# A decoder layer on one core: the orders of all engines rearranged, the second batch projected in the prologue

## The reference

```python
# self-attention: 16 heads of 64, two null keys and values per head, q and k normalized, ALiBi, causal
xn = (x - mu) * rsqrt(var + eps) * gamma
q, k, v = heads(xn @ w_q), heads(xn @ w_k), heads(xn @ w_v)
k, v = concat([null_k, k]), concat([null_v, v])
q, k = l2norm(q) * q_scale, l2norm(k) * k_scale
attn = softmax(masked(8.0 * q @ k.T - slope[h] * distance))
x1 = layernorm(x + (attn @ v) @ w_out)
# cross-attention: 16 heads of 8, 64 context rows per batch
x2 = layernorm(x1 + mha(x1, ctx, wq, wk, wv) @ wo.T + bo)
# two linear layers in a row, other weights for every pair of batches
x3 = layernorm(x2 + (x2 @ W1[g].T + b1[g]) @ W2[g].T + b2[g])
```

## Time and profile before

| | |
|---|---|
| median of three runs | 1048.96 us (1045.95 to 1051.13) |
| profiled execution, its own time | 1049.69 us |
| its span, first to last instruction | 1047.6 us |
| mean granted TensorE clock | 0.912 of full speed |
| busy share: TensorE, VectorE, ScalarE, GpSimd | 82%, 74%, 64%, 41% |

### The profile page before, as it was taken

How to read it: one execution, slowest core, us unless ns; L and a number is a source line. 1 busy time by engine, 2 the same in 40 slices (tenths; PEclk the granted TensorE clock), 3 DMA queues, 4 the chain that set the end, 5 groups by cost and what they waited for, 6 DMA issues and landing times. The chain is left out here.

```text
span 1047.6 us, 19543 instructions
## 1 busy us (share of the span) xinstructions
PE 856.9 (82%) x6469; PEld 609.2 (58%) x6469; DVE 772.6 (74%) x2496; ACT 671.2 (64%) x2002; POOL 424.7 (41%) x356
## 2 busy tenths in 40 slices
PE   6778788797888879787887979888797978887763
PEld 4546566475655647565565747556474755656542
DVE  6554677878788787878778787887878787676744
ACT  5485768567585856758485765848576684756532
POOL 1134272625345162535416362542626254162511
PEclk8789999899999989989999998989999898989875
DMA  5000000000100001000100001000010000000000
GB/s 183 6 6 2 11 21 12 6 12 1 27 11 6 12 6 32 1 11 7 26 12 6 12 6 29 4 6 12 6 32 6 7 1 26 6 6 6 7 1 10
DMA packets 26418, 15.62 MB, mean 15 GB/s; under 512 B 4304, under 2 KB 25552, under 8 KB 26320
## 3 DMA queue, kind: packets, MB, share of 16 engines
q1 hardware_dynamic: 26320, 14.38, 4.8%
HBM read 12.27 MB, written 2.10 MB: 14 GB/s over the span
## 5 line engine op out<-in xcount | busy, mean ns | idle before, releaser
L1580 POOL TENSOR_TENSOR pr<-pr,rden 128x512 f32<-128x512 f32 x192 | 193.2, 1040 | 138.5 <-DVE rden L1037 138.5
L1347 ACT ACTIVATE pr<-pr,nmin 128x256 f32<-128x256 f32 (+1 forms) x512 | 225.5, 443 | 13.6 <-DVE nmin L1022 13.5
L1022 DVE CUSTOM_DVE_ANT_0 pr<-psS,alibi,nullmin 128x256 f32<-128x256 f32 (+1 forms) x512 | 180.5, 413 | 16.6 <-PE psS L553 16.6
L553 PE MATMUL psS<-kT,qT 64*128 64x256 f32 (+1 forms) x1024 | 121.6, 368 | 33.5 <-DVE nmin L1022 33.3
L1377 ACT ACTIVATE xp<-xp 128x1024 f32<-128x1024 f32 x32 | 33.8, 1057 | 152.2 <-DVE xp L1082 152.2
L1571 POOL TENSOR_TENSOR qk<-qk,rn 128x1024 f32<-128x1024 f32 x64 | 120.5, 1906 | 25.1 <-DVE rn L883 25.1
L575 PE MATMUL psT<-ident,pr 128*128 128x128 f32 x768 | 126.7, 293 | 1.5 <-POOL pr L1580 1.5
L978 DVE TENSOR_REDUCE ssq<-sq 128x16 f32<-128x1024 f32 x64 | 77.9, 1218 | 62.6 <-ACT sq L1313 62.2
L553 PEld LDWEIGHTS psS<-kT,qT 64*128 64x128 f32 x1024 | 85.3, 201 | 63.3 <-issue 60.1
L1613 POOL TENSOR_TENSOR x1b<-x,bo 128x256 f32<-128x256 f32 x16 | 11.7, 734 | 244.6 <-DVE r L1094 222.7
L1305 ACT ACTIVATE qk<-psJ 128x512 f32<-128x512 f32 x128 | 76.0, 596 | 48.7 <-PE psJ L443 48.5
(11 more groups left out here) (145 smaller groups left out, 1762.1 us busy)
## 6 DMA issues: line engine op xcount, KB each, us to landing
w1s<-w1b SPq DMA_DIRECT2D x8, 258.0 KB, 3.1
xin<-x SPq DMA_DIRECT2D x16, 128.0 KB, 2.2
xres<-x SPq DMA_DIRECT2D x16, 128.0 KB, 2.1
w2s<-w2T SPq DMA_DIRECT2D x8, 256.0 KB, 3.5
out<-x SPq DMA_DIRECT2D x16, 128.0 KB, 1.8
pr<-w_kv SPq DMA_DIRECT2D x2, 512.0 KB, 5.5
pr<-w_q SPq DMA_DIRECT2D x1, 512.0 KB, 3.9
wo<-wout SPq DMA_DIRECT2D x1, 512.0 KB, 6.0
```

The source lines that it names most:

```text
L553: mm = pe.matmul(psS[score_bank(t, c)][:, keys * j:keys * (j + 1)], qT[r, h // 2, P * t:P * (t + 1)], kT[r, h // 2, 0:keys], start=True, s ...
L1022: dve.tensor_tensor_reduce(pr[t][:, h, :], psS[score_bank(t, c)][:, keys * j:keys * (j + 1)], alibi[:, h, SEQ - keys:SEQ], 1.0, nullmin[:, ...
L1347: act.activation(pr[t][:, h, :], pr[t][:, h, :], ACT.Exp, bias=nmin[:, t, h:h + 1], scale=-1.0, accum_out=dparts[:, t, h, 0:1]).then_inc(e ...
L1580: pool.tensor_tensor(pr[t][:, hs, :], pr[t][:, hs, :], rden[:, t, hs].unsqueeze(2).broadcast_to([P, heads, P * (t + 1)]), ALU.mult).then_i ...
```

## The change

Nothing is computed otherwise. What is changed is the order in which the engines' queues hold the steps, and what the prologue does:

- VectorE: `ln3_begin` and `ln3_end` stand earlier among the first tile's masks; `ln4_end` stands ahead of `denominators(i, 1)`, not behind; `ln1_end` stands ahead of the cross denominators; the second tile's sums of squares of batch i + 1 and its `norms` stand among the masks of the second tile; half of the ALiBi rows are made here.
- ScalarE: seeds, the q and k copies and the squares of batch i + 2 stand earlier; `x1T` is copied first.
- GpSimd: `norm_qk(i + 1, 0)` stands behind `norm_probs(i, 0)` (it stood ahead of it), `norm_qk(i + 1, 1)` at the end of the iteration.
- TensorE: `project_qk(i + 2, 1)` to `(i + 2, 4)` stand one or two steps earlier.
- Batch 1's `ln1`, projections, copies, squares and first norms stand in the prologue on all engines, where they stood in iteration 0. Its input has a buffer of its own (`xin1`, in the memory of `r2`) and its own DMA, and `p` holds for iteration 0 too.

```diff
-            return i + 3 < NB, i + 2 < NB, i + 1 < NB, i >= 1, i >= 2, 1 <= i < NB - 1
+            return i + 3 < NB, i + 2 < NB, i + 1 < NB, i >= 1, i >= 2, i + 1 < NB
...
             sp.dma_start(wqk_raw[:, HD:2 * HD], w_kv[:, 0:HD]).then_inc(wk_loaded, 16)
+            sp.dma_start(xin1[:], x_dram[:, 1]).then_inc(xin1_loaded, 16)
...
             turn_null_keys()
+            xn_turn(1)
+            for c in range(4):
+                project_qk(1, c)
             merged_nulls()
             null_values()
             project_nulls(0)
+            for c in range(4, QK_CHUNKS):
+                project_qk(1, c)
             project_v(0, 0)
...
                 if i == 0:
-                    for k in range(2, QK_CHUNKS):
-                        project_qk(1, k)
-                    project_nulls(1)
                     context_kv()
...
+                    if f and k == 4:
+                        project_qk(i + 2, 1)
...
             def iteration(i, w, g):
                 d, f, a, c, e, p = stages(i)
-                if i == 0:
-                    split_xnT(1)
                 if e:
                     add_y2(i - 2)
+                    ln3_begin(i - 2)
+                need(dve, probsT_ready, PC * (i - 1) + TILE_PC[0])
+                mask_scores(i, 0, (0, 1))
+                if e:
+                    ln3_end(i - 2)
+                mask_scores(i, 0, (2, 3))
+                null_shift(i, 0)
                 if p:
                     sum_squares(i + 1, 1, 0)
-                need(dve, probsT_ready, PC * (i - 1) + TILE_PC[0])
-                mask_scores(i, 0, (0, 1))
-                if p:
-                    sum_squares(i + 1, 1, 1)
-                    floor_squares(1)
-                if e:
-                    ln3_begin(i - 2)
-                mask_scores(i, 0, (2, 3))
-                null_shift(i, 0)
-                if e:
-                    ln3_end(i - 2)
-                if p:
-                    norms(i + 1, 1)
-                if i == 0:
-                    ln1_begin(2)
-                    ln1_end(2)
                 need(dve, probsT_ready, PC * i)
                 for k in range(8):
                     mask_scores(i, 1, (k,))
                     if k == 1:
+                        if p:
+                            sum_squares(i + 1, 1, 1)
+                            floor_squares(1)
                         denominators(i, 0)
+                    if k == 4 and p:
+                        norms(i + 1, 1)
...
                 null_shift(i, 1)
-                denominators(i, 1)
                 if e:
                     ln4_end(i - 2)
+                denominators(i, 1)
                 if c:
                     cross_shift(i - 1, 0)
                     cross_shift(i - 1, 1)
...
                 if f:
                     split_xnT(i + 2)
+                if d:
+                    ln1_begin(i + 3)
...
-                if d:
-                    ln1_begin(i + 3)
-                copy_pT(i, 6)
+                if d:
+                    ln1_end(i + 3)
+                if a:
+                    null_scores(i + 1)
                 if c:
                     cross_denominators(i - 1, 0)
...
-                copy_pT(i, 5)
-                copy_pnT(i, 1)
-                if c:
-                    cross_exponentials(i - 1, 1)
-                if f:
-                    copy_qk(i + 2, 0)
                 if d:
                     ln_seed("ln1", (0, 1), i + 4)
-                copy_pT(i, 7)
+                copy_pnT(i, 1)
+                copy_pT(i, 5)
+                if f:
+                    copy_qk(i + 2, 0)
+                if c:
+                    cross_exponentials(i - 1, 1)
...
                 if c:
                     x1_plus_bias(i - 1)
-                if p:
-                    norm_qk(i + 1, 0)
                 if e:
                     x2_plus_bias(i - 2, (i - 2) // 2)
                 norm_probs(i, 0)
                 if p:
-                    norm_qk(i + 1, 1)
+                    norm_qk(i + 1, 0)
                 if c:
                     spread_values(i)
                 norm_probs(i, 1)
...
                 spread_keys(i)
                 if c:
                     norm_cross(i - 1)
+                if p:
+                    norm_qk(i + 1, 1)
```

More of the change, by code:

```diff
@@ L210, in program @@
         r3 = r2
+        xin1 = r2
         x3 = sb("x3", [P, NT, P])
@@ L716, in _ @@
             project_nulls(0)
+            for c in range(4, QK_CHUNKS):
+                project_qk(1, c)
             project_v(0, 0)
             project_v(0, 1)
[L719 to L723, removed]
+            for c in range(4):
+                turn_qk(0, 2 * c)
+                turn_qk(0, 2 * c + 1)
+                if c < 2:
+                    project_v(0, 2 + c)
+            project_nulls(1)
             def iteration(i, w, g):
                 d, f, a, c, e, p = stages(i)
-                if i == 0:
-                    xn_turn(1)
                 scores(i, 0, 0)
@@ L802, in iteration @@
                         if f:
[L803 to L805 removed]
+                            project_qk(i + 2, 4)
                 if c:
@@ L896, in ln_end, with make_alibi @@
                 return last
+            def make_alibi(heads):
+                dve.wait_ge(a_loaded, 16)
+                for h in heads:
+                    dve.tensor_scalar(alibi[:, h, :], dist, float(slopes()[h]), None, ALU.mult).then_inc(alibi_ready_dve, 1)
             def scale_rows():
@@ L961, in ln1_begin @@
             def ln1_begin(n):
-                dve.wait_ge(xin_loaded, 16 * (n + 1))
-                ln_begin("ln1", xin, (0, 1), n + 1)
+                if n == 1:
+                    dve.wait_ge(xin1_loaded, 16)
+                else:
+                    dve.wait_ge(xin_loaded, 16 * max(n, 1))
+                ln_begin("ln1", xin1 if n == 1 else xin, (0, 1), n + 1)
             def ln1_end(n):
-                ln_end("ln1", xin, xn, (0, 1), n + 1).then_inc(xn_ready, 1)
+                ln_end("ln1", xin1 if n == 1 else xin, xn, (0, 1), n + 1).then_inc(xn_ready, 1)
             def split_xnT(n):
@@ L1123, in _ @@
             split_wqk(3)
+            ln1_begin(1)
             null_squares()
             norm_null_keys()
+            ln1_end(1)
             sum_squares(0, 0, 0)
-            split_wv(0)
+            split_xnT(1)
+            make_alibi(range(8, H))
             sum_squares(0, 0, 1)
             floor_squares(0)
+            norms(0, 0)
+            split_wv(0)
+            sum_squares(0, 1, 0)
             split_wv(1)
-            norms(0, 0)
-            sum_squares(0, 1, 0)
-            split_wn()
             sum_squares(0, 1, 1)
             floor_squares(1)
+            split_wn()
             norms(0, 1)
@@ L1410, in _ @@
             copy_qk(0, 3)
-            null_keys_seed()
             copy_qk(0, 4)
             copy_qk(0, 5)
+            null_keys_seed()
             square_qk(0, 0, 0)
             copy_qk(0, 6)
+            ln_seed("ln1", (0, 1), 2)
             square_qk(0, 0, 1)
@@ L1420, in _ @@
             square_qk(0, 1, 0)
+            for c in range(4):
+                copy_qk(1, c)
             square_qk(0, 1, 1)
@@ L1423, in _ @@
             copy_nullraw(0)
-            make_alibi(range(8, H))
+            copy_qk(1, 4)
+            copy_qk(1, 5)
+            square_qk(1, 0, 0)
+            copy_qk(1, 6)
+            copy_qk(1, 7)
+            square_qk(1, 0, 1)
             copy_v(0, 0)
             copy_v(0, 1)
+            ln_seed("ln1", (0, 1), 3)
+            qk_seed(1, 0)
             act.wait_ge(kscale_ready, 1)
@@ L1431, in _ @@
                     copy_v(0, 2 + k)
-            ln_seed("ln1", (0, 1), 2)
+            square_qk(1, 1, 0)
+            square_qk(1, 1, 1)
+            copy_nullraw(1)
             def iteration(i, w, g):
                 d, f, a, c, e, p = stages(i)
+                if e:
+                    ln_seed("ln3", (0, 1), i - 1)
+                if c:
+                    copy_x1T(i - 1)
                 if a:
                     copy_v(i + 1, 0)
-                exponentials(i, 0, (0,))
-                if c:
-                    copy_x1T(i - 1)
-                exponentials(i, 0, (1,))
-                if i == 0:
-                    copy_qk(1, 0)
-                    copy_qk(1, 1)
+                exponentials(i, 0, (0, 1))
                 if a:
                     copy_v(i + 1, 1)
-                if p:
-                    qk_seed(i + 1, 1)
-                if e:
-                    ln_seed("ln3", (0, 1), i - 1)
                 if c:
@@ L1640, in iteration @@
                 if i == 0:
-                    norm_qk(1, 0)
-                    norm_qk(1, 1)
                     spread_values(i)
```

85 lines of the change are left out of this document (32 added, 53 removed).

## The result

The changed kernel takes 976.16 us, the median of four runs (973.33 to 977.13), against 1050.05 for the kernel before; the ratio is 0.930, with a 95% interval of 0.926 to 0.933. The forecast was 980 us, from 952 to 1015. The profiled execution has a span of 975.3 us, 72.3 less than before.

| stretch | before | after | difference | forecast |
|---|---|---|---|---|
| up to the first scores of iteration 2 | 172.8 | 164.4 | -8.4 | -4.5 |
| first halves, iterations 2 to 13, mean | 24.98 | 25.30 | 12 x 0.32 = +3.9 | 0 |
| second halves, even ones, mean | 35.26 | 30.82 | 6 x -4.44 = -26.6 | with the odd ones |
| second halves, odd ones, mean | 36.71 | 31.46 | 6 x -5.25 = -31.5 | -58.8 |
| from the first scores of iteration 14 to the end | 143.3 | 133.6 | -9.7 | -6.8 |

The account below looks back on a forecast made before the run. No engine is busy throughout; the one large loss was TensorE's 3.40 us wait for xp, as GpSimd holds VectorE's ln4_end. Gains 58.8 + 6.8 + 0 + 4.5 = 70.1 us from 1049.7 give 980 us, range 952 to 1015.

Parts of the forecast that it names:

- The main step: Second halves: ln4_end ahead of denominators(1) ends TensorE's wait for xp and slow running; 4.9 us, 58.8 over iterations 2 to 13.
- 4.40 and 5.85: Odd second halves' excess over iteration 1: 4.40 us, or 5.85 without iteration 1's own 1.45 us wait at merge_ffn.
- I take the 3.40 alone for each: Iterations 14 and 15, no projections behind the wait: only TensorE's 3.40 us wait each is gained, 6.8 us.
- The first half: Masks and exponentials: VectorE gains by moved steps, is held about as long, ScalarE ends as now; 0 us.
- the lower end of -5 us: First halves: ScalarE sets the half, 24.4 against 24.8 us, gaining 0.4 each; -5 us over thirteen iterations.
- the rule quoted in the prediction: VectorE and GpSimd share a port pair exclusively; operations with two SBUF inputs need it, the second to come is blocked.
- The prologue: Batch 1's work moved from iteration 0 to the prologue: 16.8 us gone, 12.3 added, net gain 4.5, ends 12 and 0.
- I take 12.3: Prologue: eight projections, the null projection and the turn of xn add 12.3 us of TensorE, the full amount.
- the lower bound of 4.9: Prologue: least time added, 4.9 us, if TensorE's 7.4 us of idle time took up part of the 12.3.
- The other side of the sum: Iteration 0: the 11.7 us context delay and VectorE's 5.05 us wait for the ln1 seed go, 16.8 us.
- The third rival: GpSimd late: norm_qk(i+1,1) behind norm_cross makes TensorE's turn_qk(i+1,4) wait; 1056 us, chance 0.05.
- the lower of the prediction's two values: GpSimd's end after norm_probs(1): 23.2 us, or 20.5 if the cross denominators come 2.7 us sooner.

Follow-up runs that it names:

- norms_late: Kernel after with norms(i + 1, 1) moved from among the second tile's masks to behind ln4_end, ahead of denominators(i, 1): 940.2 us, ratio 0.896.
- qk0_early: Kernel after with norm_qk(i + 1, 0) ahead of norm_probs(i, 0) on GpSimd, VectorE's order untouched: 943.3 us, ratio 0.901.
- prologue_alone: Prologue of the kernel after with the iterations of the kernel before, without their i == 0 pieces for batch 1: 1034.5 us, ratio 0.986.
- ln4_alone: Kernel before with one edit, ln4_end ahead of denominators(i, 1): 985.7 us, ratio 0.939.
- add_wait: Kernel before in its own order, with GpSimd's norm_probs(i, 1) also waiting until ln4_end(i - 2) is done: 992.9 us, ratio 0.948.
- qk_split: Kernel after with each norm_qk in four GpSimd instructions of 512 columns in place of two of 1024: 960.2 us, ratio 0.917.

## Why the prediction was right

*The main step.* GpSimd holds `ln4_end`, that delays `cross_shift`, and TensorE stands still and then runs slowly: shown by three kernels, one that moves the step, one that moves it back, and one that leaves it and keeps GpSimd away. The 4.9 us an iteration were 4.84 in the full change (58.1 us over twelve iterations, 58.8 forecast) and 4.52 with the move alone. In the odd iterations the full change gives 0.90 us more than the move, and TensorE's wait at `merge_ffn` is gone from it, as the prediction had it when it chose between 4.40 and 5.85. In the even ones it gives 0.25 us less, and why is not shown.

*The end.* From iteration 14 on the gain was 9.7 us, 6.8 forecast. "I take the 3.40 alone for each" was too little: iteration 14's second half fell by 4.7 us (29.68 to 24.96), and the stretch behind iteration 15's first half by 4.6 (66.71 to 62.14). TensorE had run slowly there too: `cross_scores(1)` of iteration 14 took 2.08 us before and 1.13 after.

*The first half.* The sum of nearly nothing was right, for a reason that was only half right. The prediction expected VectorE to be held for about as long as it gains by the steps that moved behind it; so it was. But it took a half of about 24.4 us for the shortest that ScalarE allows. The runs show a half of 23.1 us where `norms` is not held (norms_late, qk0_early), so the new order had 1.9 us an iteration to give (24.98 - 23.07), and the hold took 2.2 (25.30 - 23.07). Over twelve iterations that is 23 us won and 27 lost: that the two nearly cancel is luck, since neither size was forecast. (One half of 26.64 us, iteration 13, lifts the mean before from 24.83 to 24.98.) The step that failed is the lower end of -5 us, 0.4 an iteration: it went by iteration 1's 23.4 with 1 us added for a copy and two seeds, and the half can be shorter than that.

The Trainium skill, page "SBUF — State Buffer", section "Who interferes with whom", says besides the rule quoted in the prediction that a tensor_scalar may take the second port pair too, and that a tensor_reduce on this chip never does. The traces agree: the tensor_scalar of `ln4_end` was held (2.03 for 0.60 us), the sum of squares beside `norm_qk` was not (1.20, qk0_early). What the page says of the other side, that GpSimd blocks when it comes second, no run here shows: the eight `norm_probs` took 8.02 to 8.05 us with a held instruction beside them and without.

*The prologue.* The mechanism was right, the size not: 4.5 us were forecast for prologue and iteration 0, and prologue_alone measured 15 (13.0 up to iteration 1 in its trace). The term that failed is "I take 12.3": iteration 0 began 5.7 us later there. That is near the lower bound of 4.9, but not for the bound's reason. TensorE's idle time took up nothing: from 16.5 us to the first scores it was idle for 7.4 us before (busy for 19.39 of 26.83) and 7.5 in prologue_alone (24.98 of 32.53). What was too high is the price of 1.28 us for each projection, taken where the clock was low. Two of the passes in prologue_alone, of which a projection has three, in stretches with a granted clock of 0.50 (20.50 to 23.40) and 1.00 (36.66 to 39.96):

```profile
22.77 0.63 PE L445 MATMUL psJ<-wqk_hi,xnT_lo 128*128 128x512 f32 x1
...
39.56 0.40 PE L445 MATMUL psJ<-wqk_hi,xnT_lo 128*128 128x512 f32 x1
```

So a part of the gain hangs on the granted clock, which differs between kernels that hold the same prologue. In qk0_early, with the same prologue, the granted clock from 16.5 us to the first scores is 0.69, as before the change, where prologue_alone has 0.79; TensorE is busy there for 29.89 us, and iteration 0 begins 11.3 us later than before, near the 12.3. Over the seven kernels with this prologue it is 5.7 to 11.6, and 8.1 in the kernel after. The other side of the sum was nearly right: iteration 0 lost 18.7 us in its trace (73.84 to 55.16), 16.8 forecast. In the kernel after, the context is copied directly behind `aoT`, as the prediction said, at 75.7 us (ScalarE's timeline of iteration 0):

```profile
75.18 0.58 ACT L1336 ACTIVATE aoT<-psY 128x512 f32<-128x512 f32 x1
75.66 1.25 ACT L1297 ACTIVATE kTx<-psJ,xb 128x512 f32<-128x512 f32 x2
```

There iteration 1 begins 9.9 us sooner than before, not 13.0: iteration 0 starts 2.4 us later than in prologue_alone and its first half is 1.8 us longer; its `norms` is held too.

*The sum.* That 72.3 us came so near to 70.1 is in part luck too: the first halves lost 3.9 us that were forecast as nothing, and the stretch up to iteration 2 and the end gave 3.9 and 2.9 us more than forecast.

*The third rival*, GpSimd late at the turn of q and k, did not come about: `norm_qk(i + 1, 1)` ends at 549.29 in iteration 8, 20.5 us behind `norm_probs(1)`, the lower of the prediction's two values.

## What to carry to other kernels

A small VectorE instruction that runs three to ten times its usual length beside a busy GpSimd is a scheduling fault, and it can be mended from either side: move it, move GpSimd's work, or cut GpSimd's instructions smaller. Three dependent small instructions can be held by three GpSimd instructions in turn. After a change that helped, look for the same pattern at the new places: the kernel after had moved one such pair apart and put another together, and moving three more instructions is worth another 36 us (940 against 976).

## What the runs showed of the hardware beyond that

Whether an instruction was held went by what it reads. In the kernel after, no mask, which reads PSUM and one tensor in SBUF, took more than 0.49 us, and no batch statistics (`ln_st`, one tensor in SBUF) more than 0.30, beside GpSimd or away from it. But even the tensor_scalar that adds epsilon to every second number of `ln_mv`, two numbers a partition, can be held. Its usual time is 0.17 us; in VectorE's timeline of iteration 2 it runs to the end of a GpSimd instruction of `norm_probs(1)` (193.78 to 194.82):

```profile
194.21 0.63 DVE L875 TENSOR_SCALAR ln_small<-ln_mv 128x2 f32<-128x2 f32 x1
```

In iteration 8 the same instruction keeps its usual time beside `norm_probs(0)`:

```profile
518.00 0.17 DVE L875 TENSOR_SCALAR ln_small<-ln_mv 128x2 f32<-128x2 f32 x1
```

There it starts 0.07 us before a GpSimd instruction ends (517.03 to 518.07) and so has next to nothing to wait for. A usual time beside a busy GpSimd shows that an instruction escapes the hold only if it lies well inside a GpSimd instruction.

Seven of these kernels hold the same prologue (all but ln4_alone and add_wait; in qk_split only GpSimd's pieces are smaller), and yet TensorE's first scores came at 49.0 us (prologue_alone), 49.5, 51.2, 51.4, 54.6 (qk0_early), 54.7 and 55.0. What differs is the granted clock, a mean over the two levels of 1.2 and 2.4 GHz. From 16.5 to 30 us it is about the same in prologue_alone and qk0_early (0.62 and 0.64, TensorE busy for 8.5 and 7.8 of 13.5 us); then they part. Windows of prologue_alone (length, busy us of TensorE, weight load, VectorE, ScalarE and GpSimd, each with its count, then granted clock, DMA share, GB/s):

```profile
30.00:49.03 19.03, 16.51 (x100) 13.11 (x99) 11.46 (x35) 10.35 (x22) 3.76 (x2) 0.91 0.03 8
```

The same of qk0_early:

```profile
30.00:49.00 19.00, 17.40 (x78) 14.43 (x78) 7.82 (x24) 6.55 (x15) 3.76 (x2) 0.63 0.00 1
```

In the same 19 us TensorE got through 100 matmul instructions at 0.91 and 78 at 0.63, busy in both. What decides which clock an execution gets there is open. It makes up to 6 us (55.0 - 49.0), and a comparison of two kernels by a few microseconds has to allow for it.
